# Self-attention pipeline of a perceiver layer on one core: projection pieces apart from each other, the context product of a tile at the head of the next round

## The chip, the core and the metric

One core of a Trainium2 chip runs the whole kernel. The metric is the device time of one execution in microseconds (us). Each kernel is measured in several runs and the median is given. The profile and its trace come from one execution, whose own time is given beside its span (first to last instruction).

## What is computed

A perceiver layer on 16 batches of 64 latent rows of width 256, all in float32:

```
x = x + xattn(ctx_1024, layernorm(x), mask, ...)      # cross-attention, 1601 context rows
x = x + attn(layernorm(x), W_q, b_q, ...)             # causal self-attention, 16 heads of 16
x = x + ffn(layernorm(x), w1, b1, ...)                # 4 experts, 2 chosen per row
# self-attention, per batch:
q, k = rope(heads(x @ W_q.T + b_q)), rope(heads(x @ W_k.T + b_k))
v = heads(x @ W_v.T + b_v)
probs = softmax((q k^T + causal mask) / sqrt(dh))
out = (probs v) @ W_o.T + b_o
```

## The kernel before

The program has four blocks one after the other. Block 0 prepares the latents and the query/key products, block 1 is the cross-attention over 16 batches and ends at about 1529 us of the span, block 2 (`block_2`) finishes the cross-attention and does the self-attention, and block 3 is the expert network. The change is in `block_2` alone, about 1532 to 1731 us.

`block_2` treats the 1024 rows as RT = 8 tiles of 128 rows (two batches each). A tile goes through named stages. Each engine has its own function `run(name, t)` with the part that it plays in a stage, and all call `stages(run)`, so that all engines go through the same list of (stage, tile). In round s (s = -2 to 10) a stage with lag g handles tile s - g. What an engine does within a round is in the order of that list; semaphores hold it where it needs another engine. Float32 products are made from two fp32r halves: ScalarE copies a PSUM result to the high half, VectorE subtracts to get the low half, and `split_pair` (L249) issues three matmuls for each product.

- y0 to y3 (lag -2): the value projection of a tile in four pieces of 12 matmuls each. The piece goes to a PSUM bank (`y_bank`): for tiles 0 to 3 the pieces alternate between banks 1 and 7, for tiles 4 to 7 all go to bank 1. ScalarE (L1207) and VectorE (L1310) evict it to `ysplit`, of which there is one copy. Its data come in "units" of 2 MB (two pieces each) through a ring of three, loaded by SyncE (L176).
- a1 (lag -1): the output projection, 24 matmuls on `ysplit` into bank 0; VectorE adds the residual and takes moments (L1314 to L1317).
- a2n, a2 (lag 0): normalise on VectorE, two transposes on TensorE (L1423), split (L1214, L1300).
- b1, b1v (lag 0): query/key product (`late,xnT`, six matmuls) and value product (`wv_self,xnT`); bias on VectorE (L1331), rotation on GpSimd (L1278 to L1282), value mask on VectorE (L1336).
- b2 (lag 1): four transposes of the rotated rows (L1449), eviction by ScalarE.
- c1, c1m (lag 1): scores (L1461), causal mask (L1342), maximum and subtraction (L1347, L1348), exponential on ScalarE (L1227).
- c2 (lag 1): transposes of the probabilities (L1471); row sums on VectorE (L1352).
- c3 (lag 1): the context product, 16 pairs of small matmuls (L1479); VectorE scales it by the row sums (L1359).
- d1, d2 (lag 2), d3n, d3, e (lag 3): output projection and second residual, second normalisation, router logits. f (listed in `HIDDEN_AT`) is a piece of block 3's first product, put after some stages of rounds 6 to 9.

Three waits decide much of what follows. ScalarE may overwrite `ysplit` with the first piece of tile t only when a1 of tile t-1 has read it:

```python
# scalar, stage y:
act.wait_ge(S["y_full"], 4 * t + piece + 1)
if t >= 1:
    act.wait_ge(S["x1_full"], t)
# tensor, stage y:
evicted = 4 * t + piece - (1 if t < TWO_BANKS else 0)
if evicted > 0:
    pe.wait_ge(S["y_low"], evicted)
# tensor, stage a2:
pe.wait_ge(S["x1_done"], min(t + 2, RT))
```

So a piece of tiles 4 to 7 waits until the piece before it is evicted, and a2 of tile t waits until VectorE has added a1 of tile t + 1.

Of the kernel before, what the change touches and what calls it, by code (L numbers as in the profile page):

```python
# [1077 lines left out]
def block_2(nc, ins, o_scratch, w_scratch, bank, x2, xn2T, E, W, ctx):  # L1078
# [52 lines left out]
    def stages(run):  # L1131

        for s in range(-2, RT + 3):
            for name, lag in (("d3n", 3), ("a2n", 0), ("a1", -1), ("b2", 1), ("y0", -2), ("d3", 3), ("a2", 0), ("c1", 1),
                              ("y1", -2), ("d1", 2), ("b1", 0), ("c1m", 1), ("b1v", 0), ("d2", 2), ("y2", -2), ("c2", 1),
                              ("y3", -2), ("e", 3), ("c3", 1)):
                if 0 <= s - lag < RT:
                    run(name, s - lag)
                if (s, name) in HIDDEN_AT:
                    run("f", HIDDEN_AT.index((s, name)))  # L1140
# [56 lines left out]
    def _(act):  # L1197
        def run(name, t):
# [49 lines left out]
            if name == "d3":  # L1248
                act.wait_ge(S["xn2T_full"], t + 1)
                act.activation(xn2T[:, :, 0, t * P:(t + 1) * P], bank[7][:, 0:D].rearrange("p (k x) -> p k x", k=KD),  # L1250
                               ACT.Copy).then_inc(S["xn2T_high"], 1)
        stages(run)

    @block.gpsimd
    def _(pool):
# [8 lines left out]
        def run(name, t):  # L1264
# [24 lines left out]
            if name == "d2":  # L1289
                moments(1, z, t, "d_stat", "d_rstd")  # L1290
        stages(run)

    @block.vector
    def _(dve):
# [7 lines left out]
        def run(name, t):  # L1302
# [78 lines left out]
            if name == "d3":  # L1381
                dve.wait_ge(S["xn2T_high"], t + 1)
                low(xn2T[:, :, 1, t * P:(t + 1) * P], bank[7][:, 0:D].rearrange("p (k x) -> p k x", k=KD),
                    xn2T[:, :, 0, t * P:(t + 1) * P], "xn2T_low")
        stages(run)

    @block.tensor
# [502 lines left out]
```

## Time and profile before

| | us |
|---|---|
| median of 3 runs | 1918.56 |
| the three runs | 1912.68, 1918.58, 1918.56 |
| the profiled execution, own time | 1919.26 |
| its span | 1917.5 |
| TensorE busy | 1814.2 (95% of the span) |
| VectorE busy | 1339.9 (70%) |
| ScalarE busy | 952.2 (50%) |
| GpSimd busy | 603.2 (31%) |
| mean granted TensorE clock | 0.986 of full |

Busy shares are averages over four blocks. To read the stretch that the change touches, take the timeline of TensorE from 1532 to 1731 us: each line there is a run of matmuls of one kind, and the bracket behind it is the time that the engine stood idle before it, and what released it.

### The profile page before, as it was taken

The page shows a single profiled execution, that of the slowest core. Times are in us where ns is not written, and L with a number is a line of the kernel's source. Part 1 is how long each engine was busy: PE and PEld are TensorE (multiplying, and loading weights), DVE is VectorE, ACT ScalarE, POOL GpSimd, SP SyncE. Part 2 cuts the span into 40 slices and gives each one's busy share as a digit, 9 for nine tenths or more (in the row PEclk, how much of TensorE's full clock was granted, in tenths as well). Part 3 has the DMA queues.
Part 4 walks back from the last instruction along what each step waited for, and adds up shares of the span by engine and source line. Part 5 has one row for each costly group of instructions (what it writes and reads, how often), then busy time and mean ns, then how long its engine had stood idle before and what let it go on. Part 6 is the DMA issues. An engine that isn't in the chain of part 4 may idle for free. (4 is left out here: it accounts for less than half of the span.)

```text
span 1917.5 us, 32020 instructions
## 1 busy us (share of the span) xinstructions
PE 1814.2 (95%) x10259; PEld 1582.9 (83%) x10259; DVE 1339.9 (70%) x3147; ACT 952.2 (50%) x1665; POOL 603.2 (31%) x647
## 2 busy tenths in 40 slices
PE   5889999999999999999999999999999978888998
PEld 4678888888888888888888888888888777866886
DVE  7577767677777767676777777776776437667666
ACT  4545555555545455555555464545454323334444
POOL 3424334251615151434324151515150014430000
PEclk9989999999999999999999999999999989899999
DMA  8822313131313222331313131322221495501231
GB/s 278 290 57 83 114 37 115 46 103 46 103 47 103 81 70 85 97 95 54 114 37 112 46 103 46 103 71 81 79 90 50 170 389 220 178 2 78 89 114 39
DMA packets 125421, 197.24 MB, mean 103 GB/s; under 512 B 71568, under 2 KB 95024, under 8 KB 119216
## 3 DMA queue, kind: packets, MB, share of 16 engines
q1 hardware_dynamic: 125360, 196.45, 30.7%
q8 instruction: 36, 0.59, 0.1%
q14 instruction: 25, 0.20, 0.0%
HBM read 123.01 MB, written 73.42 MB: 102 GB/s over the span
## 5 line engine op out<-in xcount | busy, mean ns | idle before, releaser
L249 PE MATMUL o_bank<-probT,val 128*128 128x512 f32 x2496 | 685.2, 410 | 7.5 <-DVE probT L887 5.0
L249 PE MATMUL s_bank<-late,qkT 128*128 128x416 f32 x3072 | 627.8, 355 | 12.3 <-DVE qkT L892 10.4
L249 PEld LDWEIGHTS s_bank<-late,qkT 128*128 128x128 f32 x3072 | 572.0, 189 | 42.7 <-issue 11.6
L249 PEld LDWEIGHTS o_bank<-probT,val 128*128 128x128 f32 x2496 | 439.4, 189 | 90.0 <-DVE probT L887 11.6
L851 ACT ACTIVATE prob<-prob,negmax 128x1665 f32<-128x1665 f32 x128 | 216.2, 1689 | 379.4 <-DVE negmax L916 379.4
L887 DVE TENSOR_TENSOR probT<-t_bank,probT 128x512 fp32r<-128x512 f32 x416 | 283.2, 687 | 145.4 <-ACT probT L829 140.5
L829 ACT ACTIVATE probT<-t_bank 128x512 fp32r<-128x512 f32 x416 | 242.6, 591 | 224.0 <-PE t_bank L968 223.7
L911 DVE CUSTOM_DVE_ANT_0 prob<-s_bank,bias 128x416 f32<-128x416 f32 x512 | 296.1, 585 | 69.2 <-PE s_bank L249 68.0
L968 PE MATMUL t_bank<-ident,prob 128*128 128x128 f32 x1664 | 250.9, 274 | 10.4 <-DVE probT L887 6.4
L968 PEld LDWEIGHTS t_bank<-ident,prob 128*128 128x128 f32 x1664 | 205.9, 141 | 51.2 <-DVE probT L887 13.6
L805 POOL TENSOR_TENSOR late_y<-w_raw,late_y 128x1280 fp32r<-128x1280 f32 x16 | 48.2, 3012 | 397.4 <-ACT late_y L823 397.4
L923 DVE TENSOR_SCALAR prob<-prob,rsum 128x1665 f32<-128x1665 f32 x128 | 165.9, 1296 | 4.6
L393 POOL TENSOR_TENSOR stage<-stage 128x1024 f32<-128x1024 f32 x48 | 125.9, 2623 | 34.6 <-ACT stage L338 34.6
L892 DVE TENSOR_TENSOR qkT<-qk,qkT 128x256 fp32r<-128x256 f32 x128 | 56.3, 440 | 108.2 <-ACT qkT L835 108.2
L394 POOL TENSOR_TENSOR stage<-stage,g 128x1024 f32<-128x1024 f32 x48 | 125.0, 2603 | 3.8
L338 ACT ACTIVATE stage<-stage,shift,rstd 128x256 f32<-128x256 f32 x224 | 120.0, 593 | 1.6 <-POOL shift L375 1.2
L249 PE MATMUL late_bank<-xn2T,ffn_w 128*128 128x512 f32 x384 | 93.5, 400 | 2.3 <-ACT stage L1624 1.3
L899 DVE TENSOR_TENSOR late<-s_bank,late 128x512 fp32r<-128x512 f32 (+1 forms) x128 | 69.4, 584 | 36.5 <-ACT late L847 36.5
L249 PEld LDWEIGHTS late_bank<-xn2T,ffn_w 128*128 128x128 f32 x384 | 72.7, 192 | 18.8 <-ACT stage L1624 2.7
L364 POOL TENSOR_TENSOR small<-stats 128x9 f32<-128x9 f32 (+1 forms) x32 | 6.7, 210 | 246.3 <-DVE stats L330 246.3
L330 DVE BATCH_NORM_STATS2 stats<-stage 128x6 f32<-128x256 f32 x224 | 78.7, 412 | 0.0
L847 ACT ACTIVATE late<-s_bank 128x512 fp32r<-128x512 f32 (+1 forms) x128 | 60.5, 526 | 21.4 <-PE s_bank L982 21.4
(209 smaller groups left out, 1916.6 us busy)
## 6 DMA issues: line engine op xcount, KB each, us to landing
o_scratch<-outT SPq DMA_DIRECT2D x32, 1024.0 KB, 4.8
stage<-in_ctx SPq DMA_DIRECT2D x48, 512.0 KB, 3.9
w_scratch<-late_y SPq DMA_DIRECT2D x16, 1280.0 KB, 6.4
ffn_w<-o_scratch SPq DMA_DIRECT2D x10, 2048.0 KB, 9.0
qk<-qk_scratch SPq DMA_DIRECT2D x16, 1024.0 KB, 6.8
ffn_w<-w_scratch SPq DMA_DIRECT2D x16, 1024.0 KB, 7.2
late_y<-o_scratch SPq DMA_DIRECT2D x6, 2048.0 KB, 10.7
w_raw<-in_wall SPq DMA_DIRECT2D x16, 640.0 KB, 7.1
```

The source lines that it names most:

```text
L249: mm = pe.matmul(out, weights(a), moving(b), start=first and n == 0, stop=last and n == 2)
L330: dve.bn_stats(self.stats[:, STAT[c], :], self.raw[:, c, :]).then_inc(self.stat_done, 1)
L338: act.activation(self.raw[s, c, :], self.raw[s, c, :], ACT.Identity, bias=self.shift[s, m:m + 1], scale=self.rstd[s, m:m + 1]).then_inc(se ...
L393: link(eng.tensor_tensor(rows, rows, raw[:, 13:14, :].to_broadcast([P, 4, D]), ALU.subtract))
L394: eng.tensor_tensor(rows, rows, g1[:, :].unsqueeze(1).to_broadcast([P, 4, D]), ALU.mult).then_inc(self.keys_done, 1)
L829: act.activation(probT[:, slot, 0, :], bank[:, :], ACT.Copy).then_inc(t_high, 1)
L851: act.activation(prob[:, i, :], prob[:, i, :], ACT.Exp, bias=negmax[:, i:i + 1], accum_out=psum_[:, i:i + 1]).then_inc(exp_done, 1)
L887: dve.tensor_tensor(probT[:, slot, 1, :], bank[:, :], probT[:, slot, 0, :].bitcast(F32), ALU.subtract).then_inc(t_done, 1)
L899: dve.tensor_tensor(keyT[:, k, 1, a * P:z * P], bank[:, at:at + (z - a) * P], keyT[:, k, 0, a * P:z * P].bitcast(F32), ALU.subtract).then_ ...
L911: apart(dve.tensor_tensor_reduce(out=prob[:, i, s], in0=s_bank[j][:, 0:QTR], in1=W["bias"][:, s], scale=1.0, scalar=NEG, op0=ALU.add, op1= ...
L923: dve.tensor_scalar(prob[:, i, :], prob[:, i, :], rsum[:, i:i + 1], None, ALU.mult).then_inc(prob_done, 1)
L968: mm = pe.transpose(bank[:, t * P:(t + 1) * P], prob[:, 4 * h + t, c * P:(c + 1) * P], ident[:, :])
```

## The change

The list in `stages` is put in another order. No operation, tile shape, buffer or semaphore is added or taken away.

```diff
         for s in range(-2, RT + 3):
-            for name, lag in (("d3n", 3), ("a2n", 0), ("a1", -1), ("b2", 1), ("y0", -2), ("d3", 3), ("a2", 0), ("c1", 1),
-                              ("y1", -2), ("d1", 2), ("b1", 0), ("c1m", 1), ("b1v", 0), ("d2", 2), ("y2", -2), ("c2", 1),
-                              ("y3", -2), ("e", 3), ("c3", 1)):
+            for name, lag in (("d3n", 3), ("a2n", 0), ("b2", 1), ("c3", 2), ("y0", -2), ("a1", -1), ("y1", -2), ("d3", 3), ("a2", 0),
+                              ("c1", 1), ("d1", 2), ("b1", 0), ("c1m", 1), ("y2", -2), ("b1v", 0), ("d2", 2), ("c2", 1),
+                              ("y3", -2), ("e", 3)):
```

Four things move: y0 goes from behind a1 to ahead of it, y1 from behind c1 to directly behind a1, y2 from behind d2 to ahead of b1v and d2, and c3 from the end of a round to behind b2 of the next one (its lag goes from 1 to 2).

TensorE at the seam of rounds 2 and 3 (`ffn_w1,wv` and `late_y,wv` are pieces y of the value projection, `late,ysplit` is a1, `vblk,pt` is c3, `ident,stage` into bank 2 is b2 and into bank 0 is a2, `ident,xn2` is d3). Before:

```order
L249 MATMUL late_bank1<-late_y,wv 128x256 x12
L1479 MATMUL late_bank5<-vblk,pt 64x32 x16
L249 MATMUL late_bank0<-late,ysplit 128x256 x24
L1449 MATMUL late_bank2<-ident,stage 128x128 x4
L249 MATMUL late_bank1<-ffn_w1,wv 128x256 x12
L1501 MATMUL late_bank7<-ident,xn2 128x128 x2
L1423 MATMUL late_bank0<-ident,stage 128x128 x2
```

And with the change, from the same piece y3 on:

```order
L249 MATMUL late_bank1<-late_y,wv 128x256 x12
L1449 MATMUL late_bank2<-ident,stage 128x128 x4
L1479 MATMUL late_bank5<-vblk,pt 64x32 x16
L249 MATMUL late_bank1<-ffn_w1,wv 128x256 x12
L249 MATMUL late_bank0<-late,ysplit 128x256 x24
L249 MATMUL late_bank1<-ffn_w1,wv 128x256 x12
L1501 MATMUL late_bank7<-ident,xn2 128x128 x2
L1423 MATMUL late_bank0<-ident,stage 128x128 x2
```

Behind y3 now stand b2, c3 and y0 before a1; behind a1 stands y1, which writes the same bank 1 as y0.

VectorE in the second half of round 3 (`mx` and `sc<-sc,mx` are c1m, `vblk` is b1v, the three `x2`/`st2`/`mv2` rows are d2, `sm` and `rsm` are c2, `att` is c3's scaling, and `ysplit<-late_bank1` are low halves of pieces y). Before:

```order
L1347 TENSOR_REDUCE mx<-sc 128x16
L1348 TENSOR_TENSOR sc<-sc,mx 128x1024
L1336 TENSOR_TENSOR vblk<-late_bank3,vmask 128x512
L1367 TENSOR_TENSOR x2<-late_bank7,x2 128x256
L1369 BN_STATS st2<-x2 128x6
L1370 BN_AGGR mv2<-st2 128x2
L1310 TENSOR_TENSOR ysplit<-late_bank1,ysplit 64x256 x2
L1352 TENSOR_REDUCE sm<-sc 128x16
L1353 RECIPROCAL rsm<-sm 128x16
L1310 TENSOR_TENSOR ysplit<-late_bank1,ysplit 64x256 x2
L1359 TENSOR_TENSOR att<-late_bank5,rsm 128x256
```

With the change:

```order
L1347 TENSOR_REDUCE mx<-sc 128x16
L1348 TENSOR_TENSOR sc<-sc,mx 128x1024
L1310 TENSOR_TENSOR ysplit<-late_bank1,ysplit 64x256 x2
L1336 TENSOR_TENSOR vblk<-late_bank3,vmask 128x512
L1367 TENSOR_TENSOR x2<-late_bank7,x2 128x256
L1369 BN_STATS st2<-x2 128x6
L1370 BN_AGGR mv2<-st2 128x2
L1352 TENSOR_REDUCE sm<-sc 128x16
L1353 RECIPROCAL rsm<-sm 128x16
L1310 TENSOR_TENSOR ysplit<-late_bank1,ysplit 64x256 x2
```

The low half of y2 now stands ahead of b1v and d2 instead of behind them.

## Rows read from the trace of the kernel before

**Rows 1.** Waits of TensorE, 1530 to 1740 us: total us, times, longest.
```profile
PE late_bank L1471 <- ACT sc L1227: 8.1, 7, 1.8
PE late_bank L249 <- DVE ysplit L1310: 7.8, 10, 1.8
```

**Rows 2.** Timeline of TensorE, start of b1 in rounds 0 to 6: start, us, what.
```profile
1568.08 1.67 PE L249 MATMUL late_bank<-late,xnT 128*128 128x512 f32 x6 [0.84 <-DVE xnT L1300]
...
1584.73 1.67 PE L249 MATMUL late_bank<-late,xnT 128*128 128x512 f32 x6
...
1603.85 1.65 PE L249 MATMUL late_bank<-late,xnT 128*128 128x512 f32 x6
...
1623.75 1.65 PE L249 MATMUL late_bank<-late,xnT 128*128 128x512 f32 x6
...
1643.68 1.65 PE L249 MATMUL late_bank<-late,xnT 128*128 128x512 f32 x6
...
1667.90 1.64 PE L249 MATMUL late_bank<-late,xnT 128*128 128x512 f32 x6
...
1685.60 1.67 PE L249 MATMUL late_bank<-late,xnT 128*128 128x512 f32 x6 [0.25 <-DVE xnT L1300]
```

**Rows 3.** The same view, round 3 and the head of round 4.
```profile
1615.31 3.12 PE L249 MATMUL late_bank<-late,ysplit 128*128 128x256 f32 x24 [0.74 <-issue]
...
1618.62 1.65 PE L249 MATMUL late_bank<-ffn_w,wv 128*128 128x256 f32 x12
...
1622.11 1.66 PE L249 MATMUL late_bank<-ffn_w,wv 128*128 128x256 f32 x12 [0.78 <-DVE ysplit L1310]
...
1630.12 1.09 PE L1471 MATMUL late_bank<-ident,sc 128*128 128x128 f32 x8 [1.18 <-ACT sc L1227]
1631.76 1.66 PE L249 MATMUL late_bank<-ffn_w,wv 128*128 128x256 f32 x12 [0.55 <-DVE ysplit L1310]
...
1635.22 3.11 PE L249 MATMUL late_bank<-late,ysplit 128*128 128x256 f32 x24 [0.17 <-issue]
```

**Rows 4.** Timeline of VectorE, round 3.
```profile
1618.46 0.42 DVE L1314 TENSOR_TENSOR x<-late_bank,stage 128x256 f32<-128x256 f32 x1 [2.15 <-PE late_bank L249]
...
1621.11 0.85 DVE L1310 TENSOR_TENSOR ysplit<-late_bank,ysplit 64x256 fp32r<-64x256 f32 x2 [1.54 <-ACT ysplit L1207]
...
1622.53 0.68 DVE L1300 TENSOR_TENSOR xnT<-late_bank,xnT 128x512 fp32r<-128x512 f32 x1
...
1628.90 0.68 DVE L1336 TENSOR_TENSOR vblk<-late_bank,vmask 128x512 f32<-128x512 f32 x1
...
1630.75 0.86 DVE L1310 TENSOR_TENSOR ysplit<-late_bank,ysplit 64x256 fp32r<-64x256 f32 x2 [0.17 <-ACT ysplit L1207]
1631.64 1.22 DVE L1352 TENSOR_REDUCE sm<-sc 128x16 f32<-128x1024 f32 x1
```

**Rows 5.** Timeline of ScalarE, round 3.
```profile
1620.31 0.77 ACT L1207 ACTIVATE ysplit<-late_bank 64x256 fp32r<-64x256 f32 x2 [0.30 <-PE late_bank L249]
```

**Rows 6.** Timeline of GpSimd: the last rotation of tile 0.
```profile
1574.06 0.72 POOL L1282 TENSOR_TENSOR stage<-rs,rc 128x256 f32<-128x256 f32 x1
```

**Rows 7.** DMA issues, 1546 to 1547 us: KB, median us from issue to landing.
```profile
ffn_w<-o_scratch SPq DMA_DIRECT2D x1, 2048.0 KB, 13.6
```

**Rows 8.** Timeline of TensorE: a1 of rounds 0, 1 and 5.
```profile
1561.07 3.12 PE L249 MATMUL late_bank<-late,ysplit 128*128 128x256 f32 x24 [1.79 <-issue]
...
1575.78 4.60 PE L249 MATMUL late_bank<-late,ysplit 128*128 128x256 f32 x24 [1.79 <-issue]
...
1657.23 5.32 PE L249 MATMUL late_bank<-late,ysplit 128*128 128x256 f32 x24
```

**Rows 9.** Stretch: us, busy of PE, PEld, DVE, ACT, POOL; granted clock, DMA share, GB/s.
```profile
1655.00:1660.00 5.00, 5.00 (x48) 4.92 (x48) 1.91 (x5) 0.17 (x1) 0.00 (x0) 0.50 0.92 307
```

**Rows 10.** Timeline of TensorE: d3 and the piece f behind it, round 9.
```profile
1720.42 0.69 PE L1501 MATMUL late_bank<-ident,xn 128*128 128x128 f32 x2 [0.91 <-DVE xn L1375]
1720.76 2.91 PE L249 MATMUL late_bank<-xn2T,ffn_w 128*128 128x512 f32 x6
```

## The prediction

> **What bounds the kernel now.** I read the waits of TensorE first, then its timeline through `block_2`, then VectorE, ScalarE and GpSimd in the same round, then the DMA issues and the granted clock by stretch. The change touches about 200 us of 1917.5; outside them nothing is reordered, so I take the other blocks as they are. Inside, TensorE sets the pace: its two largest waits are 8.1 us for the exponential ahead of c2 and 7.8 us for evictions of pieces y [rows 1]. The start of b1 is my marker of a round. From it to the next b1 the kernel takes 16.65, 19.12, 19.90, 19.93, 24.22 and 17.70 us [rows 2]. So an undisturbed full round (rounds 2 to 5) is 19.9 us. Of these TensorE stands still 0.74 or 0.17 ahead of a1, 0.78 ahead of y1, 1.18 ahead of c2 and 0.55 ahead of y3 [rows 3], some 2.7 us.
>
> The first wait to price is the eviction of a piece y. y0 ends at 1618.62 + 1.65 = 1620.27 and y1 starts at 1622.11 [rows 3]: 1.84 us, made of 0.77 on ScalarE [rows 5], 0.85 on VectorE [rows 4] and 0.2 of hand-over. In the first rounds the same price stands bare ahead of a1, 1.79 each time [rows 8]. This is what the new order is placed to fill: b2, c3 and y0 now stand between y3 and a1.
>
> **The change part by part.** Rounds are counted from their b1.
>
> *Tail of a full round.* Before, c2 starts at 6.37 and y3 at 8.01 after b1 [rows 2, 3]. The low half of y1 (0.85) is no longer on VectorE's queue ahead of the maximum, but the bias waits for TensorE's own product (1.65), so I grant 0.25: c2 at 6.1. ScalarE still does the exponential ahead of y2's high half, so VectorE's low half of y2 ends at 7.6 instead of 7.86 [rows 4], y3 starts at 7.7 and ends at 9.3. What changes is behind it on VectorE: b1v and d2, which ran during the exponential (1628.90 to the end of the busy stretch at 1630.58 [rows 4], 1.7 us), now wait behind that low half. They end at 9.4, the row sum (1.22 [rows 4]) and reciprocal (0.25) at 10.9, the low half of y3 at 11.8. Whoever waits for y3 starts at 11.85; a1 started at 11.47 (1635.22 [rows 3]). e, b2 and c3 lie ahead of that moment and cost nothing by themselves: a wait of about 0.5 remains behind them. This step costs 0.4.
>
> *y0 ahead of a1.* y0 runs 11.85 to 13.35, a1 from there, ending 3.11 later at 16.46 [rows 3]. y0 cannot be evicted meanwhile, because `ysplit` is still read by a1. For tiles 4 to 7 (rounds 2 to 5) y1 goes to the same bank 1, so it waits for that eviction: 1.84 bare, y1 at 18.3. Before, b2 stood there and y1 had y0, a2 and c1 beside the eviction, with 0.78 left. This is the main loss.
>
> *y1 ahead of a2.* y1 ends at 19.9. ScalarE and VectorE must evict it, then d3's and a2's transposes, in that order. From ScalarE's start on a piece y to the end of the low half of `xnT` the trace has 1620.31 to 1623.21 [rows 4, 5], 2.9 us, 0.2 of it the router weights that only round 3 splits. So b1 starts at 19.9 + 2.7 + 0.05 = 22.65. d3, a2, c1 and d1 (about 1.4 us of work) are all that TensorE has beside it. Before, y1 stood between c1 and d1 and covered this.
>
> Round: 22.65 - 19.9 = **+2.75 us**, for the steps into rounds 3, 4 and 5: 8.25. The step into round 2 has no d3 and starts from the shorter round 1: I work it the same way to 21.25 against 19.12, +2.15.
>
> *Early rounds.* The three bare waits of 1.79 go, but little comes of it. In round -1 and 0 the units arrive late: the unit for tile 2 is issued at 1546.49 and lands 13.6 us later [rows 7], at 1560.1, and y0 of tile 2 is now first and must wait for it; before, a1 filled that time, at 1561.07 [rows 8]. Then a2 of round 0 waits for a1's sum, which VectorE does behind the low half of y0: 0.04 + 0.77 + 0.03 + 0.85 + 0.42 + 0.15, 2.25 after a1's end, of which y1 covers 1.5. So: y0 from 1560.2, a1 from 1561.7 to 1564.8, y1 to 1566.3, a2 at 1567.2, its split behind that of y1, and b1 of round 0 at 1569.3 for 1568.08: **+1.2**. In round 1, b2 is first and waits for the rotation, which ended at 1574.78 [rows 6], 6.7 after b1, when y3 is done at 6.0: 0.7. The wait ahead of a2 and the split behind y1 come again. I get 16.25 from b1 to b1, where before had 16.65 with a1 at 4.60 instead of 3.12 [rows 8], 15.15 without that: **+1.1** at equal clock.
>
> *End.* In round 6 there is no piece y; c3 and a1 now stand between b2 and c1 and cover c1's wait for b2's eviction, while a2 waits a little longer; I work the step to 17.25 for 17.70 [rows 2]: -0.45. In round 9 c3 covers d3's wait (0.91 [rows 10]): -0.9. Rounds 7 and 8 stay, their d3 being paced by GpSimd.
>
> *c3's lag* adds no copy; its operands are double, and c1 waits for its scaling only after y0, a1 and y1. Nothing. SyncE's loads hang on y1 and y3 of older tiles; from round 1 on they are issued about a round or more (17 us, [rows 2]) ahead of their use, which is more than the 13.6 that one takes [rows 7]: nothing.
>
> *Clock.* The chip granted 0.50, which is 1.2 GHz, in 1655 to 1660 [rows 9], behind the waits at c2 and y3 of round 4; a1 took 5.32 instead of 3.11 [rows 8], and the step was 24.22 instead of 19.9: 4.3. The slow a1 of round 1 cost 1.5. So 5.8 us of this execution are low clock between rounds 1 and 5. With the change, TensorE stands still 5.5 us of 22.65 in a full round (0.5, 1.84, about 1.4, 1.0, 0.7), against 2.7 of 19.9, so I do not expect less low clock; I take it as equal, with both ends in the range: none (-5.8) and two more stretches like the long one (+8.6). The Trainium skill (TensorE: Matmul & The Clock Gate, section on HAM oscillation) puts the penalty at throttled time times one minus the clock ratio. By it the long stretch of some 10.4 us would cost 5.2, not the 4.3 of the rows, since part of it falls on waits; by the page each further stretch would add 0.9 more than I count.
>
> **The sum** at equal clock: +1.2 + 1.1 + 2.15 + 8.25 - 0.45 - 0.9 = +11.35. The profiled execution took 1919.26, its span and 1.8 around it, so 1930.6; it stands 0.7 above the median of the three runs, 1918.56. The prediction is 1918.56 + 11.4 = **1930.0**.
>
> **Rivals.**
> *The clock holds (not slower).* If a1, no longer right behind a bare wait, keeps TensorE at 2.4 GHz through rounds 1 to 5 and the end, the time falls by 5.8 and by another 2.5 there (f took 2.91 [rows 10], six matmuls of this size otherwise 1.65 [rows 2], and a second piece f did the same): 1930.0 - 5.8 - 2.5 = 1921.7, within 0.3% of before. It decides from the point where no row in 1560 to 1730 shows a granted clock of 0.50. For it: the run of 1912.68, 5.9 below the others, just the size of the low stretches. Against it: twice the standing time in a round. 0.10.
>
> *Low clock in most full rounds.* TensorE now stands still ahead of y1 and b1 too, in each of rounds 2 to 5. The price is 4.3 each for three more rounds: 1942.9. The same page of the Trainium skill has it that throttled is the default state and activity releases it (section "What's actually happening"); by that rule this is where the added idle time leads. One round in four went this way in the trace. 0.17.
>
> *The wait ahead of y1 is not bare.* If y0's eviction passed during a1, rounds 2 to 5 would each give 1.84 back and a2 in rounds 0 and 1 some 0.8 together: 1930.0 - 8.2 = 1921.8. Against it: the wait on `x1_full` is in the code. 0.05. With a full clock on top, 1913: the only way I see to faster, 0.03.
>
> **How the numbers follow.** Forecast 0.65, for 1924.3 to 1938.6; 0.3% is 5.8 us, about what a measurement of this kernel can tell from no change. Slower by more: 0.65 + 0.17 = 0.82. Within: 0.10 + 0.05 = 0.15. Faster: 0.03. The range, 1920 to 1940, takes in the two cases at 1921.7 and 1921.8 and up to two more low stretches, and leaves out 0.17 + 0.03 = 0.20.
>
> **What would show it.** Right: y1 of tiles 4 to 7 starts 1.8 us after a1's end, released by VectorE on `ysplit`; a wait of about 0.4 and one of 0.5 to 1 around d1 ahead of b1; b1 to b1 22.6 at full clock; no wait ahead of a1; VectorE idle about 1.9 ahead of y2's low half. Wrong: rounds under 20.5, or y1 starting directly behind a1; or a granted clock that differs from before by more than the two long stretches.

## Result and profile after

| | before | with the change |
|---|---|---|
| median, us | 1918.07 (6 runs, 1912.68 to 1919.18) | 1926.47 (6 runs, 1923.07 to 1928.06) |
| profiled execution, own time | 1919.26 | 1925.98 |
| its span | 1917.5 | 1924.2 |
| mean granted TensorE clock | 0.986 | 0.988 |

The ratio over the runs is 1.0056, with a 95% interval of 1.0041 to 1.0071, so the kernel is slower. The size depends on how it is taken: 8.4 us between the medians (a ratio of 1.0044), 6.7 between the profiled executions, some 10.7 by the ratio. Forecast were 1930.0 and slower.

TensorE's waits with the change, 1530 to 1745 us (total us, times, longest), against [rows 1]:

```profile
PE late_bank L249 <- DVE ysplit L1310: 11.7, 12, 1.9
PE late_bank L249 <- DMA ffn_w<-o_scratch: 8.8, 3, 5.9
PE late_bank L1471 <- ACT sc L1227: 7.3, 8, 1.5
PE late_bank L249 <- DVE xnT L1300: 4.6, 5, 1.6
...
PE late_bank L1489 <- DVE xn2T L1300: 2.9, 4, 1.2
```

Two more lines of the same view of before belong beside these:

```profile
PE late_bank L249 <- issue: 5.4, 6, 1.8
PE late_bank L249 <- DMA ffn_w<-o_scratch: 4.5, 1, 4.5
```

The change did remove what it was aimed at: the 5.4 us of before are the six waits ahead of a1 ("issue" means that the view names no releaser), and none of them is left. But the waits for the eviction of pieces y grew from 7.8 to 11.7 us, and the waits on split transposes grew from 1.3 to 4.6 us ahead of b1 and from 1.0 to 2.9 ahead of d1. The DMA wait grew by 4.3 us. Of these, 2.8 come from the new order: y0 now stands first in rounds -1 and 0 and waits there for its unit (1.75 at 1548.14 and 1.09 at 1560.72). The other 1.5 do not: the first pieces y, whose order is unchanged, took 3.10 us in this execution and 4.59 in that of before, so TensorE was earlier at the same wait.

The markers of [rows 2], b1 in rounds 0 to 6, in TensorE's timeline of the changed kernel:

```profile
1569.69 2.93 PE L249 MATMUL late_bank<-late,xnT 128*128 128x512 f32 x6 [1.64 <-DVE xnT L1300]
...
1587.06 1.67 PE L249 MATMUL late_bank<-late,xnT 128*128 128x512 f32 x6 [1.06 <-DVE xnT L1300]
...
1608.14 1.67 PE L249 MATMUL late_bank<-late,xnT 128*128 128x512 f32 x6 [1.26 <-DVE xnT L1300]
...
1631.07 1.67 PE L249 MATMUL late_bank<-late,xnT 128*128 128x512 f32 x6
...
1653.46 1.67 PE L249 MATMUL late_bank<-late,xnT 128*128 128x512 f32 x6
...
1676.94 1.67 PE L249 MATMUL late_bank<-late,xnT 128*128 128x512 f32 x6
...
1693.86 1.67 PE L249 MATMUL late_bank<-late,xnT 128*128 128x512 f32 x6 [0.38 <-DVE xnT L1300]
```

From b1 to b1 this is 17.37, 21.08, 22.93, 22.39, 23.48 and 16.92 us, where before had 16.65, 19.12, 19.90, 19.93, 24.22 and 17.70. The step into round 4 (22.39) shows a full round with no low clock in it. Its TensorE rows answer to [rows 3]:

```profile
1642.55 1.67 PE L249 MATMUL late_bank<-late_y,wv 128*128 128x256 f32 x12
1644.05 3.03 PE L249 MATMUL late_bank<-late,ysplit 128*128 128x256 f32 x24
1648.98 1.68 PE L249 MATMUL late_bank<-late_y,wv 128*128 128x256 f32 x12 [1.90 <-DVE ysplit L1310]
...
1652.95 0.41 PE L1489 MATMUL late_bank<-ident,att 128*128 128x128 f32 x2 [1.24 <-DVE xn2T L1300]
1653.46 1.67 PE L249 MATMUL late_bank<-late,xnT 128*128 128x512 f32 x6
...
1659.45 1.09 PE L1471 MATMUL late_bank<-ident,sc 128*128 128x128 f32 x8 [0.77 <-ACT sc L1227]
1661.09 1.67 PE L249 MATMUL late_bank<-ffn_w,wv 128*128 128x256 f32 x12 [0.55 <-DVE ysplit L1310]
```

y0 and a1 run with no wait. Then TensorE stands for 1.90 us until y0 is evicted, and after y1 for 1.24 until the transposes behind y1 are split. This second wait shows ahead of d1; b1 follows d1 at once. ScalarE and VectorE around round 3 show why (against [rows 4] and [rows 5]). On ScalarE, the copy of y0's high half:

```profile
1624.24 0.77 ACT L1207 ACTIVATE ysplit<-late_bank 64x256 fp32r<-64x256 f32 x2 [4.86 <-PE late_bank L249]
```

On VectorE:

```profile
1625.04 0.86 DVE L1310 TENSOR_TENSOR ysplit<-late_bank,ysplit 64x256 fp32r<-64x256 f32 x2 [4.36 <-ACT ysplit L1207]
1625.93 0.42 DVE L1314 TENSOR_TENSOR x<-late_bank,stage 128x256 f32<-128x256 f32 x1
...
1628.90 0.86 DVE L1310 TENSOR_TENSOR ysplit<-late_bank,ysplit 64x256 fp32r<-64x256 f32 x2 [1.87 <-ACT ysplit L1207]
...
1637.71 0.86 DVE L1310 TENSOR_TENSOR ysplit<-late_bank,ysplit 64x256 fp32r<-64x256 f32 x2 [1.78 <-ACT ysplit L1207]
...
1640.12 0.18 DVE L1370 BATCH_NORM_AGGREGATE mv<-st 128x2 f32<-128x6 f32 x1
1640.21 1.19 DVE L1352 TENSOR_REDUCE sm<-sc 128x16 f32<-128x1024 f32 x1
```

y0 was ready at 1621.28 (1619.61 + 1.67), but ScalarE's copy begins at 1624.24, 0.1 us after the end of a1 (1621.11 + 3.03), as the wait on `x1_full` demands. So VectorE is idle for 4.36 us before it can do y0's low half. It is idle for another 1.78 ahead of y2's low half, while ScalarE does the exponential and then y2's high half.

### The profile page after: what moved, and what is told of

It reads as the page before. It is cut to its first block and busy times, and to the rows that moved or that the text cites. A ratio compares the mean times of both kernels' runs of the same rounds, so it can differ in the third digit from the quotient of the medians.

```text
span 1924.2 us, 32020 instructions
## 1 busy us (share of the span) xinstructions
PE 1813.9 (94%) x10259; PEld 1577.9 (82%) x10259; DVE 1338.9 (70%) x3147; ACT 952.5 (50%) x1665; POOL 603.9 (31%) x647
## 5 line engine op out<-in xcount | busy, mean ns | idle before, releaser
L1310 DVE TENSOR_TENSOR ysplit<-late_bank,ysplit 64x256 fp32r<-64x256 f32 x64 | 26.6, 415 | 67.7 <-ACT ysplit L1207 67.3
```

## The experiments

Three readings stood against each other at first. A: the loss is y0's eviction, bare (with no work of TensorE beside it) between a1 and y1, and y1 no longer covering a2's split. B: it is VectorE's queue, with c3's scaling at the head and y2's low half ahead of b1v and d2. C: the order is neutral and the clock made the difference. Each kernel is compared with runs of before on the chip that it ran on. The changed kernel itself was not measured again beside them, so its variants are held against it by their rounds from b1 to b1. The median of before was 1913.84 for c3_head, y01_only, halves_after and bank7_after, 1915.48 for y1_back, halves_head and best, and 1914.50 for y2_only and halves_before.

### c3_head: b2 and c3 to the head, the pieces y as before

```diff
-            for name, lag in (("d3n", 3), ("a2n", 0), ("a1", -1), ("b2", 1), ("y0", -2), ("d3", 3), ("a2", 0), ("c1", 1),
+            for name, lag in (("d3n", 3), ("a2n", 0), ("b2", 1), ("c3", 2), ("a1", -1), ("y0", -2), ("d3", 3), ("a2", 0), ("c1", 1),
...
-                              ("y3", -2), ("e", 3), ("c3", 1)):
+                              ("y3", -2), ("e", 3)):
```

> The order of before, with b2 and c3 (one tile later) at the head of the round, ahead of a1; y0, y1 and y2 stay where they were. Theory A (the loss comes from the eviction of y0, bare between a1 and y1, and from y1 no longer covering a2's split): nothing of that is here, b2 and c3 fill the wait ahead of a1; full rounds of 19.6 to 19.9 us from b1 to b1 at full clock, about 1915 us. Theory B (the loss comes from VectorE's queue, c3's scaling at the head and the low half of y2): rounds over 20.5, about 1921 or more. Theory C (order is neutral and the granted clock made the difference): rounds of 19.9, time within 3 us of before.

Measured: 1913.0, ratio 0.9994 (0.998 to 1.0008), so no change of the time is shown. Steps of 19.51, 19.80 and 19.80 us into rounds 3, 4 and 5:

```profile
1621.04 1.66 PE L249 MATMUL late_bank<-late,xnT 128*128 128x512 f32 x6
...
1629.05 1.66 PE L249 MATMUL late_bank<-ffn_w,wv 128*128 128x256 f32 x12 [0.55 <-DVE ysplit L1310]
...
1631.73 1.12 PE L1479 MATMUL late_bank<-vblk,pt 128*64 128x32 f32 x32
1632.78 3.14 PE L249 MATMUL late_bank<-late,ysplit 128*128 128x256 f32 x24
```

c3 stands ahead of a1, and a1 has no wait. The half of B that is c3's scaling falls: the new places of b2 and c3 cost nothing and save 0.1 to 0.4 a round. The other half, y2's low half, is not touched by this run; y2_only, below, takes it alone.

### y01_only: only y0 and y1 moved, with b2 ahead of both

```diff
-            for name, lag in (("d3n", 3), ("a2n", 0), ("a1", -1), ("b2", 1), ("y0", -2), ("d3", 3), ("a2", 0), ("c1", 1),
-                              ("y1", -2), ("d1", 2), ("b1", 0), ("c1m", 1), ("b1v", 0), ("d2", 2), ("y2", -2), ("c2", 1),
+            for name, lag in (("d3n", 3), ("a2n", 0), ("b2", 1), ("y0", -2), ("a1", -1), ("y1", -2), ("d3", 3), ("a2", 0),
+                              ("c1", 1), ("d1", 2), ("b1", 0), ("c1m", 1), ("b1v", 0), ("d2", 2), ("y2", -2), ("c2", 1),
```

> Only y0 ahead of a1 and y1 behind it (b2 ahead of both); c3 stays at the end of its round and y2 behind d2, as before. Theory A: the whole loss is here: a wait of 1.9 us ahead of y1 in rounds 2 to 5, full rounds of 22.2 to 22.7, about 1926. Theory B: rounds near 20, 1918 to 1920. Theory C: rounds near 19.9 where the clock is full.

Measured: 1926.91, ratio 1.0063 (1.0049 to 1.0077), steps of 22.18 and 22.16 into rounds 4 and 5, with the same two waits:

```profile
1642.87 3.03 PE L249 MATMUL late_bank<-late,ysplit 128*128 128x256 f32 x24
1647.80 1.68 PE L249 MATMUL late_bank<-late_y,wv 128*128 128x256 f32 x12 [1.90 <-DVE ysplit L1310]
...
1651.77 0.41 PE L1489 MATMUL late_bank<-ident,att 128*128 128x128 f32 x2 [1.23 <-DVE xn2T L1300]
```

These two moves hold nearly the whole loss of a round: 22.18 of the changed kernel's 22.39, against 19.93. B as the main cause falls with that, and C as well, because these rounds have the full clock and are still 2.2 us longer than those of before.

### halves_after: the changed kernel, a shorter eviction

```diff
-                copy.then_inc(S["y_high"], 1)
...
+                                          heads_of(bank[y_bank(t, piece)])[rows, :, u, :], ACT.Copy).then_inc(S["y_high"], 1)
...
-                dve.wait_ge(S["y_high"], 4 * t + piece + 1)
                 for u in range(2):
+                    dve.wait_ge(S["y_high"], 8 * t + 2 * piece + u + 1)
```

> The changed kernel, with ScalarE's two copies of a piece y signalled one by one, so that VectorE's first subtraction runs beside ScalarE's second copy. Theory A: each bare eviction falls from 1.9 to about 1.5, and a2's split and y3's start come 0.4 earlier each: full rounds of 21.2 to 21.5, about 1922. Theories B and C: rounds stay at 22.4 within 0.3, about 1926.

Measured: 1918.04, ratio 1.0020 (1.0010 to 1.0029). In the seam of rounds 3 and 4 ScalarE's copies start at 1642.38 and VectorE's at 1642.79, beside the second copy, and y1's wait falls to 1.51:

```profile
1642.79 0.86 DVE L1309 TENSOR_TENSOR ysplit<-late_bank,ysplit 64x256 fp32r<-64x256 f32 x2 [3.97 <-ACT ysplit L1207]
```

```profile
1643.79 1.67 PE L249 MATMUL late_bank<-late_y,wv 128*128 128x256 f32 x12 [1.51 <-DVE ysplit L1309]
```

The steps into rounds 4 and 5 are 21.29 and 21.27, as A has it: 0.4 off the eviction is 1.1 off the round, since the round meets it ahead of y1, in the split behind y1 and ahead of y3. The time is 4 us below the 1922 that I expected. The profiled execution is 8.2 us below that of the changed kernel. Of these, 3.0 lie ahead of b1 of round 2 (1.5 of them ahead of round 0), and 1.6 are slow rows of the changed kernel in rounds 2 and 4 that this execution did not have.

### bank7_after: the changed kernel, y0 and y1 in two banks

```diff
-        return (1, 7)[piece % 2] if t < TWO_BANKS else 1
+        return (1, 7)[piece % 2] if t < TWO_BANKS else (7, 1, 1, 1)[piece]
...
-                evicted = 4 * t + piece - (1 if t < TWO_BANKS else 0)
+                evicted = 4 * t + piece - (1 if t < TWO_BANKS or piece == 1 else 0)
+                if t == TWO_BANKS and piece == 1:
+                    evicted = 4 * t - 1
...
+                if piece == 0 and t > TWO_BANKS:
+                    pe.wait_ge(S["x2_done"], t - TWO_BANKS)
...
-                    pe.wait_ge(S["y_low"], 4 * TWO_BANKS)
+                    pe.wait_ge(S["y_low"], 4 * TWO_BANKS + 1)
...
+                if t + 5 < RT:
+                    pe.wait_ge(S["y_low"], 4 * (t + 5) + 1)
```

> The changed kernel, with y0 of tiles 4 to 7 in bank 7 in place of bank 1, so that y1 need not wait for y0's eviction (d3 and d1, which use bank 7, wait for it). Theory A: the wait of 1.9 ahead of y1 goes; a wait of 0.7 ahead of a2 comes, because VectorE adds a1 behind the low half of y0; full rounds of 21.0, about 1921. Theories B and C: rounds stay at 22.4, about 1926.

Measured: 1917.93, ratio 1.0014 (1.0006 to 1.0023), steps of 20.70 into rounds 4 and 5 (21.0 and about 1921 were expected). The seam of rounds 2 and 3:

```profile
1619.76 3.04 PE L249 MATMUL late_bank<-late,ysplit 128*128 128x256 f32 x24
1622.64 1.59 PE L249 MATMUL late_bank<-ffn_w,wv 128*128 128x256 f32 x12
1624.70 0.41 PE L1507 MATMUL late_bank<-ident,xn 128*128 128x128 f32 x2 [0.47 <-DVE ysplit L1310]
...
1627.23 0.41 PE L1493 MATMUL late_bank<-ident,att 128*128 128x128 f32 x2 [1.09 <-DVE xn2T L1300]
```

y1 follows a1 at once: the wait of 1.90 was that of one bank. Another wait takes a part of its place, but not ahead of a2 as I expected: it stands ahead of d3, which shares bank 7 with y0 (0.47). The wait around d1 stays.

### y1_back: the changed kernel, y1 behind c1 again

```diff
-            for name, lag in (("d3n", 3), ("a2n", 0), ("b2", 1), ("c3", 2), ("y0", -2), ("a1", -1), ("y1", -2), ("d3", 3), ("a2", 0),
-                              ("c1", 1), ("d1", 2), ("b1", 0), ("c1m", 1), ("y2", -2), ("b1v", 0), ("d2", 2), ("c2", 1),
-                              ("y3", -2), ("e", 3)):
+            for name, lag in (("d3n", 3), ("a2n", 0), ("b2", 1), ("c3", 2), ("y0", -2), ("a1", -1), ("d3", 3), ("a2", 0),
+                              ("c1", 1), ("y1", -2), ("d1", 2), ("b1", 0), ("c1m", 1), ("y2", -2), ("b1v", 0), ("d2", 2),
+                              ("c2", 1), ("y3", -2), ("e", 3)):
```

> The changed kernel, with y1 put back behind c1; y0 ahead of a1, c3, b2 and y2 as in the change. Theory A: y1's wait of 1.9 goes, as d3, a2 and c1 stand beside y0's eviction, but these three now meet the wait for a1's sum (2.2 us after a1's end, because VectorE does the low half of y0 first), which y1 had covered: a wait of 1.8 to 2.0 ahead of a2, none ahead of b1. Full rounds of 20.8 to 21.1 in place of 22.4, about 1920. Theory D (only y1's place matters, y0 ahead of a1 is free): rounds of 19.6 to 19.9, about 1915.

A fourth reading, D, stood here: only y1's place matters, and y0 ahead of a1 is free.

Measured: 1921.71, ratio 1.0031 (1.0020 to 1.0042), steps of 21.58 and 21.31 into rounds 4 and 5. The first begins with a slow b1 (2.30 us for 1.65); the second is 0.2 above the range that I expected. The wait is where it was expected, ahead of a2:

```profile
1622.34 3.04 PE L249 MATMUL late_bank<-late,ysplit 128*128 128x256 f32 x24
1625.22 0.38 PE L1501 MATMUL late_bank<-ident,xn 128*128 128x128 f32 x2
1627.69 0.41 PE L1423 MATMUL late_bank<-ident,stage 128*128 128x128 f32 x2 [2.09 <-issue]
```

VectorE did y0's low half first (1626.28) and a1's sum after it (1627.16 to 1627.58), and a2 starts 0.1 later (1627.69). So D falls: y0 ahead of a1 is not free wherever y1 stands. One of the two waits is bare: y0's eviction ahead of y1, or a1's sum ahead of a2.

### y2_only: y2 alone ahead of b1v and d2

```diff
-                              ("y1", -2), ("d1", 2), ("b1", 0), ("c1m", 1), ("b1v", 0), ("d2", 2), ("y2", -2), ("c2", 1),
+                              ("y1", -2), ("d1", 2), ("b1", 0), ("c1m", 1), ("y2", -2), ("b1v", 0), ("d2", 2), ("c2", 1),
```

> The kernel before with y2 alone moved ahead of b1v and d2. The prediction priced the VectorE queue behind it (b1v and d2 pushed out of the exponential's shadow) at 0.4 us a round; if that holds, a1 starts 0.4 later, full rounds take 20.3 and the time is some 2 us above before. If VectorE's instructions overlap at their joints, as the trace of the changed kernel suggests (y0 started 11.47 after b1 there, as a1 did before), rounds stay at 19.9 and the time is that of before within 1 us.

Measured: 1916.07, ratio 1.0004 (0.9993 to 1.0014), which does not settle it, but the rounds do: 20.24, 20.26 and 20.23 for 19.90 to 19.93, with 0.3 more ahead of a1 than in [rows 3]:

```profile
1604.30 1.65 PE L249 MATMUL late_bank<-late,xnT 128*128 128x512 f32 x6
...
1616.09 3.11 PE L249 MATMUL late_bank<-late,ysplit 128*128 128x256 f32 x24 [1.07 <-issue]
```

a1 starts 11.79 after b1 instead of 11.47. So in the order of before the queue behind y2's low half does cost, 0.3 where I expected 0.4. Over these three or four rounds that is about 1 us, which this interval cannot tell from nothing.

### halves_before, halves_head and best: what the waits are worth

halves_before has the edit of halves_after on the kernel before, halves_head has it on c3_head. best adds to halves_head the place of d3 and the banks:

```diff
-            for name, lag in (("d3n", 3), ("a2n", 0), ("b2", 1), ("c3", 2), ("a1", -1), ("y0", -2), ("d3", 3), ("a2", 0),
+            for name, lag in (("d3n", 3), ("a2n", 0), ("b2", 1), ("c3", 2), ("d3", 3), ("a1", -1), ("y0", -2), ("a2", 0),
...
+        return (1, 7)[piece % 2] if t < TWO_BANKS else (7, 1, 1, 7)[piece]
...
+                evicted = 4 * t + piece - (1 if t < TWO_BANKS or piece % 2 else 0) - (1 if t >= TWO_BANKS and piece == 1 else 0)
...
+                if piece == 0 and t > TWO_BANKS:
+                    pe.wait_ge(S["xn2T_low"], t - TWO_BANKS)
+                if piece == 3 and t >= TWO_BANKS:
+                    pe.wait_ge(S["x2_done"], t - TWO_BANKS + 1)
...
-                if t == 0:
-                    pe.wait_ge(S["y_low"], 4 * TWO_BANKS)
+                if t + TWO_BANKS < RT:
+                    pe.wait_ge(S["y_low"], 4 * (t + TWO_BANKS) + 1)
...
+                if t + TWO_BANKS < RT:
+                    pe.wait_ge(S["y_low"], 4 * (t + TWO_BANKS + 1))
```

> The kernel before, with the two copies of a piece y signalled one by one. If the waits ahead of a1, y1 and y3 are evictions, each of them falls by 0.4: full rounds of 19.1 to 19.3 in place of 19.9, the bare waits ahead of a1 1.4 in place of 1.8, some 5 us less than before. If c2's wait for the exponential grows by what they give back, rounds stay at 19.9.

> The kernel of c3_head with the two copies of a piece signalled one by one. The waits ahead of y1 and y3 (0.8 and 0.55) fall by 0.4 each: full rounds of 19.0 to 19.2 in place of 19.8, and the waits ahead of a1 in rounds -1 and 0 fall from 1.8 to 1.4: about 1910. If evictions have slack there after all, rounds stay at 19.8 and about 1913.

> The kernel of halves_head, with d3 ahead of a1 and pieces y0 and y3 of tiles 4 to 7 in bank 7: y1 no longer waits for y0 nor y3 for y2. If the one bank is what makes the pieces wait, the waits ahead of y1 and y3 go and full rounds take 18.1 to 18.6, about 1905; the wait ahead of c2 (1.2) is left. If d3, which now waits for y3's eviction, or d1, which waits for y0's, takes its place, rounds stay at 19.0 or more, about 1910.

| | median, us | ratio to before | steps into rounds 3 to 5, us |
|---|---|---|---|
| halves_before | 1907.07 | 0.9961 (0.9946 to 0.9976) | 18.44 to 19.01 |
| halves_head | 1903.53 | 0.9933 (0.9917 to 0.9950) | 18.04 to 19.11 |
| best | 1902.11 | 0.9926 (0.9909 to 0.9942) | 18.48 to 18.51 |

All three are faster than before on their chips, by under 1%, and so than the changed kernel, which is slower than before. halves_before and halves_head were faster than I had expected: steps of 19.1 to 19.3 and 19.0 to 19.2 were forecast for them, and a time of about 1910 for halves_head. Why single steps are up to 1.1 us shorter than others of the same kernel was not traced. Round 3 of best (the first row is its b1 of round 2):

```profile
1599.78 1.64 PE L249 MATMUL late_bank<-late,xnT 128*128 128x512 f32 x6
...
1606.24 1.09 PE L1474 MATMUL late_bank<-ident,sc 128*128 128x128 f32 x8 [1.24 <-ACT sc L1226]
1607.09 1.68 PE L249 MATMUL late_bank<-late_y,wv 128*128 128x256 f32 x12
...
1611.09 0.44 PE L1506 MATMUL late_bank<-ident,xn 128*128 128x128 f32 x2 [0.84 <-DVE xn L1374]
1611.31 3.11 PE L249 MATMUL late_bank<-late,ysplit 128*128 128x256 f32 x24
...
1616.60 1.69 PE L249 MATMUL late_bank<-ffn_w,wv 128*128 128x256 f32 x12
```

In the full rounds no piece y waits any more. c2's wait for the exponential is left, and d3 waits for its normalised rows, 0.84 here and 0.16 to 0.19 in the next rounds. VectorE could not write them earlier, because it waited for GpSimd's reciprocal root:

```profile
1610.62 0.41 DVE L1374 TENSOR_SCALAR xn<-x,mv,rstd 128x256 f32<-128x256 f32 x1 [0.56 <-POOL rstd L1260]
```

a1 stands behind d3 and starts 11.52 to 11.53 after its b1, where halves_head has 10.42, 11.43 and 11.16. So d3's new place gives back ahead of a1 most of what the banks win at y1 and y3: the three steps of best are together 0.5 us shorter than those of halves_head. The medians are 1.4 us apart, and the runs of the two kernels overlap. I had expected 5, for the most part because I had put halves_head 6.5 us too high. The banks without d3's new place were not run.

## Why the prediction was right, step by step

| step | forecast | measured in the profiled execution |
|---|---|---|
| up to b1 of round 0 | +1.2 | +1.6, of it 0.6 because the block began later (1532.69 for 1532.07) |
| into round 1, equal clock | +1.1 | +1.0 (17.37 less 1.26 of slow b1, against 15.15, which is 16.65 less 1.5 of slow a1) |
| into round 2 | +2.15 | +1.96 |
| into rounds 3 to 5, equal clock | +8.25 | +7.4 (three times 22.39 - 19.93) |
| into round 6 | -0.45 | -0.78 |
| from there to block 3 | -0.9 | -1.5, part of it less low clock |
| low clock in rounds 1 to 5 | 0 (5.8 in both) | -2.9 (2.9 in place of 5.8) |
| sum | +11.35 | +6.8; block 3 itself -0.1 |

**The mechanism** came as forecast. y1 waits 1.90 for the bank (forecast 1.84), b1's split is bare, a1 has no wait, and VectorE idles 1.78 ahead of y2's low half (forecast 1.9). The two waits forecast around d1 came as one of 1.24 ahead of it. In y01_only, halves_after and bank7_after the rounds come within 0.3 us of what this reading gives.

**The full round** was put at 22.65 and measured 22.39. The term that was off is the tail of the round, put at 0.4: y0 was to start 11.85 after b1 and started at 11.48, where a1 had started at 11.47 before, so in the changed kernel this step cost nothing. y2_only shows that the queue behind y2's low half is real, 0.3 in the order of before; here c2 also starts earlier, 5.99 after b1 for 6.37 (forecast 6.1), and that makes up for it. A part of the miss is that some of VectorE's rows overlap by 0.1: d2's last row ends at 1640.30 and the row sum starts at 1640.21, and y3's low half starts in the same way before the reciprocal's end. A sum of durations misses this. From y0 to b1 the forecast was 10.80 and the trace has 10.91.

**The clock** is the largest term that was mis-sized. I took equal low clock because TensorE stands still twice as long in a round. In the trace the changed kernel had less, three short stretches instead of one long and one short one: b1 of round 0 at 2.93 for 1.67, a y1 at 2.02 and one at 2.77 for 1.67. Had it been equal, the profiled execution would have come out at +9.7, 1.7 short of the sum. This is read from one execution, though, whose mean granted clock of 0.988 is as high as any of the six (0.984 to 0.988), so the 2.9 us are not shown for the median.

The prediction also gives a reason why the long stretch of before cost 4.3 us and not 5.2, half of its 10.4: part of it falls on waits. The rows do not bear this out. From the slow y3 to the end of the slow a1 the only wait that could be hidden is the 0.17 ahead of a1 [rows 3]. What they show is that the work itself did not take twice as long at a granted clock of 0.50: a1 took 5.32 us for 3.11 [rows 3, 8], 1.7 times. The rule of the Trainium skill (TensorE: Matmul & The Clock Gate, "What's actually happening") that throttled is the default and activity releases the clock had led to the rival with low clock in most full rounds; the trace does not bear that rival out, since no stretch like that of [rows 9] occurs, and the slowest of the six runs, at 1928.06, is far from its 1942.9. The full-clock rival is out too: there is low clock in rounds 0, 2 and 4 (a granted clock of 0.57 over 1671 to 1675 us), and the fastest run is 1923.07 for its 1921.7.

**The medians** differ by 8.4 and the profiled executions by 6.7: that of before lies 1.2 us above its median and that of the changed kernel 0.5 below its own. Runs of before vary more than this, from 1911.54 to 1921.08 in the 19 beside y2_only and halves_before, and its median was 1918.07 beside the changed kernel but 1913.84 to 1915.48 beside the experiments. There y01_only, which holds nearly the whole loss of a round, lost 13.1 us in the medians. So the +11.4 of the forecast lies inside what was measured, 8.4 to 13.1, and how near the 1930.0 came to 1926.47 is in part luck.

## What to carry to other kernels

In a hand-written round, moving a step ahead of another is paid by whoever reads what lies between them: look up for each moved step which buffer its eviction overwrites and who still reads it, not only what the engine itself waits for. Filling a wait with work that shares the resource waited for (here one PSUM bank and one copy of `ysplit`) moves the wait and does not fill it. Independent work (c3, b2) does fill it, but gave only the 0.1 to 0.4 us a round that this wait was worth. Shortening the chain itself (a signal for each half) gave more, 0.9 to 1.5 us a round in halves_before, since a round meets the chain in several places.

## What was not expected

The low clock came and went in a way that standing time alone does not order. c3_head, with shorter waits than the changed kernel, has a low stretch as long as that of the kernel before (some 10 us, in round 5), behind waits at c2 (1.16) and y3 (0.55) like those of round 4 there:

```profile
1670.00:1680.00 10.00, 10.00 (x74) 9.61 (x72) 2.05 (x6) 1.87 (x5) 1.15 (x3) 0.53 0.00 0
```

TensorE is busy for all 10 us of this stretch, at a mean granted clock of 0.53 (0.50, which is 1.2 GHz, up to 1679). Waits of the same length stand in the other full rounds of c3_head, which keep the full clock. The changed kernel, with waits of 1.90 and 1.24 in one round, loses at most 1.3 us to low clock in any step from b1 to b1 up to round 6. The spread of runs differs too: before spans 8.0 us over 29 runs and 9.5 over 19, c3_head 8.9 over 12 and halves_before 6.9 over 8, but the changed kernel 5.0 over 6, y2_only 2.4 over 12, y01_only 2.0 over 6 and y1_back 1.7 over 10. The length of the waits does not order this either, since y2_only has those of before and 0.3 us more. Why some orders have long low stretches and others short ones was not tried and stays open. It also means that a gain of under 5 us in kernels that vary as before and c3_head do is read from the rounds at full clock rather than from the median.
